# Attention sums turned by VectorE's block transposes instead of TensorE's, with four smaller moves beside it

## The reference

```python
q, k = _l2norm(proj(Wq)), _l2norm(proj(Wk))
v = proj(Wv)
attn = einsum('bhqd,bhkd->bhqk', q, k)
rel = pos[None, :] - pos[:, None]
mask = (rel < 0) | (rel >= WINDOW)          # WINDOW = 128
alibi = -abs(rel) * slopes[:, None, None]
attn = softmax(attn + where(mask, NEG_INF, alibi))
out = einsum('bhqk,bhkd->bhqd', attn, v).reshape(B, T, D)
x = _layernorm(x + einsum('btd,ed->bte', out, Wo))
h = gelu(einsum('bsd,hd->bsh', x, binarize(w1)) + b1)
x = _layernorm(x + einsum('bsh,dh->bsd', h, binarize(w2)) + b2)
```

## Time and profile before

| | |
|---|---|
| median of 3 runs | 369.94 us (369.66 to 370.51) |
| span of the profiled execution, first to last instruction | 368.4 us |
| TensorE busy | 353.2 us, 96% of the span, 4461 matmuls |
| VectorE busy | 308.7 us, 84% |
| ScalarE busy | 307.3 us, 83% |
| GpSimd busy | 285.4 us, 77% |
| granted TensorE clock, mean | 0.997 |

### The profile page before, as it was taken

How to read it: one execution, slowest core, us unless ns; L and a number is a source line. 1 busy time by engine, 2 the same in 40 slices (tenths; PEclk the granted TensorE clock), 3 DMA queues, 4 the chain that set the end, 5 groups by cost and what they waited for, 6 DMA issues and landing times. The chain is left out here.

```text
span 368.4 us, 13096 instructions
## 1 busy us (share of the span) xinstructions
PE 353.2 (96%) x4461; PEld 244.1 (66%) x4461; DVE 308.7 (84%) x771; ACT 307.3 (83%) x532; POOL 285.4 (77%) x440
## 2 busy tenths in 40 slices
PE   8789999999999999999999999999999999999992
PEld 5555676667766776776677677675666667667682
DVE  5977899898898898898899988879777887786775
ACT  3588888898898998898899999988888888887753
POOL 1188999889989999998999999757756856856433
PEclk9999999999999999999999999999999999999998
DMA  7678944744655646667767773303303513413113
GB/s 231 143 117 186 185 109 98 157 99 94 137 120 106 142 96 132 139 159 154 156 144 155 153 147 74 59 4 59 59 0 59 115 45 72 114 39 76 59 59 114
DMA packets 106884, 40.19 MB, mean 109 GB/s; under 512 B 92128, under 2 KB 105824, under 8 KB 106720
## 3 DMA queue, kind: packets, MB, share of 16 engines
q1 hardware_dynamic: 106848, 39.73, 49.6%
HBM read 12.72 MB, written 4.19 MB: 46 GB/s over the span
## 5 line engine op out<-in xcount | busy, mean ns | idle before, releaser
L1341 POOL TENSOR_SCALAR_AFFINE_SELECT prob<-prob 128x512 f32<-128x512 f32 x252 | 153.7, 646 | 11.1 <-ACT prob L700 11.1
L700 ACT ACTIVATE prob<-ps 128x1024 f32<-128x1024 f32 (+1 forms) x128 | 122.2, 1009 | 13.5 <-PE ps L390 13.4
L551 PE MATMUL ps<-yT,sgn 128*128 128x512 f16 x256 | 61.1, 379 | 0.0
L772 ACT ACTIVATE ps<-ps,bias,alpha 128x512 f32<-128x512 f32 x64 | 47.9, 750 | 15.6 <-PE ps L551 12.5
L421 PE MATMUL ps<-wqkv,xt 128*128 128x512 f32 x124 | 58.7, 596 | 1.2 <-DVE qkn L952 1.1
L411 PE MATMUL ps<-prob,vdiag 128*17 128x128 f32 x1024 | 51.3, 274 | 0.3
L411 PE MATMUL ps<-prob,vnext 128*17 128x128 f32 x992 | 49.9, 273 | 0.0
L1409 POOL TENSOR_TENSOR resid<-z,resid 128x256 f32 (+1 forms) x31 | 22.5, 726 | 29.9 <-DVE z L1173 29.9
L551 PEld LDWEIGHTS ps<-yT,sgn 128*128 128x128 f16 x256 | 25.0, 98 | 22.6
L390 PE MATMUL ps<-qkT 64*64 64x192 f16 (+2 forms) x1024 | 33.7, 248 | 2.8 <-DMA qkT<-parts 2.7
L454 PE MATMUL ps<-wo,oT 128*128 128x256 f32 x128 | 36.2, 405 | 0.1
(11 more groups left out here) (113 smaller groups left out, 690.2 us busy)
## 6 DMA issues: line engine op xcount, KB each, us to landing
xt<-in_xT SPq DMA_DIRECT2D x32, 128.0 KB, 2.1
resid<-in_x SPq DMA_DIRECT2D x32, 128.0 KB, 2.2
out_dram<-resid SPq DMA_DIRECT2D x7, 512.0 KB, 2.9
w<-in_w2T SPq DMA_DIRECT2D x1, 1024.0 KB, 7.7
w<-in_w1T SPq DMA_DIRECT2D x4, 256.0 KB, 3.3
w_nat<-in_w SPq DMA_DIRECT2D x4, 256.0 KB, 3.3
wqkv<-in_wqkvT SPq DMA_DIRECT2D x3, 256.0 KB, 3.9
qkT<-parts SPq DMA_TRANSPOSE x39, 4.3
```

What stands on the lines that cost most here:

```text
L551: mm = nc.tensor.matmul(ps[:, bank, :], sgn1[:, c, P * k:P * k + P], yT[:, par, a, c, :, :], start=(m == 0), stop=(m == 2 * DC - 1))
L700: nc.scalar.activation(to, scored, ACT.Exp, scale=QK_SCALE ** -2).then_inc(exp_done, 1)
L772: nc.scalar.activation(bank, bank, ACT.Gelu, bias=bias1[:, k:k + 1], scale=alpha1[:, k:k + 1]).then_inc(gelu_done, 1)
L1341: return nc.gpsimd.affine_select(out=at, in_=at, compare_op=ALU.is_ge, fill=0.0, base=-near, pattern=[[0, CH], [1 if near else -1, P]], ch ...
```

## The change

Five things change together.

1. **The sums are turned on VectorE.** `turn_sums` reads bank `OT` (128x512) and writes it to SBUF as `turned`, each 32x32 block transposed in place. `scale_sums` takes the reciprocal of the denominators, now from `turned`, multiplies (now SBUF by SBUF), and a second block transpose (128x256) makes `oT`, the left operand of the output projection. The feature order that this gives is taken up by a new order of `Wo`'s columns (`WO_SLOTS`), made on the host side with the other weight layouts. `turn_strips`, `turn_rows`, `take_strips` and `take_rows` are gone: six transposes and two copies a step.
2. **The output projection writes into bank `OT`**, into one of its two halves by the parity of the step, once the sums of the next block have been turned out of it. The weighted sums therefore wait for `resid_done` of the block before. In the last four blocks (`project_late`) it still uses `VO`. `oT` has two buffers.
3. **`double` moves from VectorE to ScalarE**, behind the root's logarithm and exponential, from step 4 on.
4. **GpSimd selects eight heads at once** (`cut_pair`): four selects of 128x1024 a step in place of eight of 128x512, each after both chunks' exponentials. The low halves come between the two pairs.
5. **One product makes both faded copies of the values** (`faded`) in place of two.

```diff
+WO_SLOTS = [SLOTS[CH * (2 * half + k) + m] for k in range(DC) for m in range(CH) for half in range(2)]
...
-        vdiag = sb("vdiag", [P, XS, H, HD + 1])
-        vnext = sb("vnext", [P, XS, H, HD + 1])
+        faded = sb("faded", [P, 2, XS, H, HD + 1])
         prob = sb("prob", [P, XS + 2, H, P])
-        strips = sb("strips", [P, CH, P])
+        turned = sb("turned", [P, H, 2 * HD])
         rden = sb("rden", [P, H])
-        otok = sb("otok", [P, D])
-        oT = sb("oT", [P, DC, P])
+        otok = sb("otok", [P, H // 2, 2, HD])
+        oT = sb("oT", [P, 2, DC, P])
...
                 if c == 0:
                     pe.wait_ge(v_ready, q + 2 if near else NB)
-                    count(pe, ot_ready, q)
+                    count(pe, sums_turned, q)
+                    count(pe, resid_done, q - 1 if not isinstance(q, int) or q < NB - 2 else 0)
-                if near:
-                    pe.wait_ge(cut_ready, (q + 1) * NC + c + 1)
-                else:
-                    pe.wait_ge(own_cut, c + 1)
+                if c % 2 == 0:
+                    if near:
+                        pe.wait_ge(cut_ready, (q + 1) * (NC // 2) + c // 2 + 1)
+                    else:
+                        pe.wait_ge(own_cut, c // 2 + 1)
                 for n in range(2 if near else 1):
                     for m in range(CH):
                         if n == 0:
-                            v, p = vdiag[:, slot, CH * c + m, :], prob[:, OWN_AT[slot], CH * c + m, :]
+                            v, p = faded[:, 0, slot, CH * c + m, :], prob[:, OWN_AT[slot], CH * c + m, :]
                         else:
-                            v, p = vnext[:, (slot + 1) % XS, CH * c + m, :], prob[:, NEAR_AT[(slot + 1) % 2], CH * c + m, :]
+                            v, p = faded[:, 1, (slot + 1) % XS, CH * c + m, :], prob[:, NEAR_AT[(slot + 1) % 2], CH * c + m, :]
...
-            def turn_strips(q):
-
-                pe.wait_ge(strips_ready, q + 1)
-                for c in range(NC):
-                    mm = nc.tensor.transpose(ps[:, OT, P * c:P * c + P], strips[:, c, :], id32[:])
-                mm.then_inc(otok_done, 1)
-
-            def turn_rows(q):
-
-                pe.wait_ge(onorm_done, q + 1)
+            def project_out(q, par):
+
+                pe.wait_ge(ot_ready, q + 1)
+                pe.wait_ge(sums_turned, q + 2)
                 for k in range(DC):
-                    mm = nc.tensor.transpose(ps[:, OT, P * k:P * k + P], otok[:, P * k:P * k + P], id32[:])
-                mm.then_inc(ot_done, 1)
-
-            def project_out(q, values, added=0):
-
-                pe.wait_ge(ot_ready, q + 1)
-                pe.wait_ge(v_ready, values)
-                count(pe, resid_done, added)
-                for k in range(DC):
-                    mm = nc.tensor.matmul(ps[:, VO, D:2 * D], oT[:, k, :], wo[:, k, :],
+                    mm = nc.tensor.matmul(ps[:, OT, D * par:D * par + D], oT[:, par, k, :], wo[:, k, :],
                                           start=(k == 0), stop=(k == DC - 1))
                 mm.then_inc(wo_done, 1)
...
+            def project_late(q):
+
+                pe.wait_ge(ot_ready, q + 1)
+                pe.wait_ge(v_ready, NB)
+                count(pe, resid_done, q if q > NB - 4 else 0)
+                for k in range(DC):
+                    mm = nc.tensor.matmul(ps[:, VO, D:2 * D], oT[:, q % 2, k, :], wo[:, k, :],
+                                          start=(k == 0), stop=(k == DC - 1))
+                mm.then_inc(wo_done, 1)
+
                 par = slot % 2
                 scores(i, 0, par, slot, both)
                 scores(i, 1, par, slot, both)
-                if out:
-                    project_out(i - 4, i + 1)
-                if strips:
-                    turn_strips(i - 3)
                 if amid:
                     amid()
                 if next3:
                     project_qk(i + 3, (slot + 3) % XS)
-                elif next1:
-                    project_v(i + 1, (slot + 1) % XS)
-                if before_rows:
-                    before_rows()
-                if strips:
-                    turn_rows(i - 3)
-                if next1 and next3 and not early:
+                if out:
+                    project_out(i - 4, par)
+                if before_values:
+                    before_values()
+                if next1 and not early:
                     project_v(i + 1, (slot + 1) % XS)
...
-            def take_strips(q):
-                act.wait_ge(pv_done, q + 1)
-                count(act, otok_done, q)
-                nc.scalar.activation(strips[:], ps[:, OT, :].rearrange("p (c t) -> p c t", c=NC),
-                                     ACT.Copy).then_inc(strips_ready, 1)
-
-            def take_rows(q):
-                act.wait_ge(ot_done, q + 1)
-                count(act, wo_done, q)
-                nc.scalar.activation(oT[:], ps[:, OT, 0:D].rearrange("p (k t) -> p k t", k=DC),
-                                     ACT.Copy).then_inc(ot_ready, 1)
-
+            def double(n, par):
+
+                done = n + 1
+                if not isinstance(n, int):
+                    done = act.to_reg(done)
+                act.wait_ge(lo_done, done)
+                nc.scalar.activation(parts[:, par, 0:H, 2:4, :], parts[:, par, 0:H, 0:2, :],
+                                     ACT.Copy).then_inc(parts_ready, 1)
+
...
+                if next2 and doubled:
+                    double(i + 2, par)
...
+            def turn_sums(q):
+
+                dve.wait_ge(pv_done, q + 1)
+                count(dve, onorm_done, q)
+                nc.vector.transpose(turned[:].rearrange("p b d -> p (b d)"), ps[:, OT, :]).then_inc(sums_turned, 1)
+
+            def scale_sums(q, par):
+
+                dve.wait_ge(sums_turned, q + 1)
+                nc.vector.reciprocal(rden[:], turned[:, :, HD]).then_inc(rden_done, 1)
+                dve.wait_ge(rden_done, q + 1)
+                count(dve, ot_ready, q)
+                nc.vector.tensor_tensor(otok[:].rearrange("p b a d -> p a b d"),
+                                        turned[:, :, 0:HD].rearrange("p (a b) d -> p a b d", a=2),
+                                        rden[:].rearrange("p (a b) -> p a b", a=2).unsqueeze(3).to_broadcast(
+                                            [P, 2, H // 2, HD]),
+                                        ALU.mult).then_inc(onorm_done, 1)
+                dve.wait_ge(onorm_done, q + 1)
+                count(dve, wo_done, q - 1)
+                nc.vector.transpose(oT[:, par].rearrange("p k t -> p (k t)"),
+                                    otok[:].rearrange("p b a d -> p (b a d)")).then_inc(ot_ready, 1)
+
             def outputs(q):
 
-                sums = ps[:, OT, :].rearrange("p (h d) -> p h d", d=32)
-                dve.wait_ge(otok_done, q + 1)
-                count(dve, onorm_done, q)
-                nc.vector.reciprocal(rden[:], sums[:, :, HD]).then_inc(rden_done, 1)
-                dve.wait_ge(rden_done, q + 1)
-                count(dve, ot_done, q)
-                nc.vector.tensor_tensor(otok[:].rearrange("p (h d) -> p h d", d=HD), sums[:, :, 0:HD],
-                                        rden[:].unsqueeze(2).to_broadcast([P, H, HD]),
-                                        ALU.mult).then_inc(onorm_done, 1)
-
-            def add_output(q):
+                turn_sums(q)
+                scale_sums(q, q % 2)
...
+                added = ps[:, VO, D:2 * D] if late else ps[:, OT, D * par:D * par + D]
+                nc.vector.tensor_tensor(resid[:, q, :], resid[:, q, :], added, ALU.add).then_inc(resid_done, 1)
...
                 v = ps[:, VO, 0:D].rearrange("p (h d) -> p h d", d=HD)
-                for to, at in ((vdiag, 0), (vnext, 1)):
-                    made = nc.vector.tensor_tensor(to[:, slot, :, 0:HD], v,
-                                                   fade[:, at, :].unsqueeze(2).to_broadcast([P, H, HD]), ALU.mult)
-                made.then_inc(v_ready, 1)
+                nc.vector.tensor_tensor(faded[:, :, slot, :, 0:HD], v.unsqueeze(1).to_broadcast([P, 2, H, HD]),
+                                        fade[:].unsqueeze(3).to_broadcast([P, 2, H, HD]), ALU.mult).then_inc(v_ready, 1)
...
                 par = slot % 2
+                turn_sums(i - 3)
                 if prev3:
                     round_of(i - 1, True, prev_ln)
                     normalise_rows(i + 2, par)
-                if out and not next3:
-                    add_output(i - 4)
-                if strips:
-                    outputs(i - 3)
-                if out and next3:
-                    add_output(i - 4)
+                scale_sums(i - 3, 1 - par)
+                add_output(i - 4, par)
                 if aside:
                     aside()
                 if next1 and not next3:
...
-                    if not double_first:
-                        fade_values(i + 1, (slot + 1) % XS)
-                if next2:
```

(30 more changed lines are left out.)

89 lines of the change are left out of this document (35 added, 54 removed).

## The result

The changed kernel takes 384.96 us, the median of 4 runs (384.62 to 385.43), beside 370.23 for the kernel before in the same session (369.66 to 372.72): ratio 1.0391, 95% interval [1.0356, 1.0426]. It is slower by 14.7 us. The profiled execution's span is 383.4 us in place of 368.4.

What follows compares the result with a forecast made beforehand. TensorE bounded the kernel before, three engines close behind; a ring through VectorE, ScalarE and GpSimd would bound the changed loop. Loop +1.5, small copies +1.5, last steps -0.5: +2.5 on 368.4, plus 1.5 to the median, 372.4 us; range 359 to 386.

Steps and rivals of the forecast that it cites:

- rival 3: Loop: L961 and half miss the ends of GpSimd's instructions in most steps; 7.75 us a step, 384 us; chance 0.15.
- TensorE, 6.50 a step: Loop: TensorE loses 0.65 us of transposes a step and gains nothing, 7.15 becomes 6.50.
- VectorE's load, 6.95 a step: Loop: 6.54 us, less 0.56 for double and 0.14 for one product, plus 1.11 for two transposes.
- GpSimd: Loop: a select of 1024 columns takes 1.11 us, about 1.08 at pace; 6.1 us a step with the low halves.
- ScalarE: Loop: loses copies of 0.58 us and smaller, gains double at 0.62; neutral off the step's end.
- The ring, 7.08 a step, mixed 7.3: Loop: half, logarithm, double, exponentials, selects, low halves, next half held by the long low half; mixed 7.1 to 7.65.
- rival 2: Loop: VectorE's load alone rules, waits do not lengthen with the select; 6.95 us a step, 362.5 us; chance 0.2.
- Loop in sum, +1.5 and +1.5 for the small copies: 25 steps of 7.3 instead of 7.24 us, +1.5; one more small ScalarE copy in five steps, +1.5.
- New waits: Loop: weighted sums wait for add_output, TensorE idles 0.6 to 0.8 us at no cost; coarser selects wanted a step later.
- The first steps: Ahead of step 4: the forecast's sum had no term for this stretch.
- The last steps, -0.5 between -3.9 and +2.2: From 222.29 to 257 us: TensorE sheds 3.9 us; VectorE's last two blocks bring 2.2 against 1.6 free.
- Rival 1: Loop: TensorE stays the bound, held instructions fall into GpSimd's gaps; steps of 6.5 to 6.6, 351 us; chance 0.15.

Runs made afterwards that it cites:

- tiny_turns_all: The changed kernel with both VectorE block transposes cut to 32 columns from block 3 on, loop included: 380.91 us.
- fine_start: The changed kernel with selects of four heads in steps 0 to 4 only, eight heads from step 5 on: 379.66 us.
- tiny_turns_end: The changed kernel with both VectorE block transposes cut to 32 columns for the last six blocks only: 382.06 us.
- early_turns: The changed kernel with VectorE turning the sums of blocks 30 and 31 earlier in the written-out end: 387.57 us.
- before_eight: The kernel before with only the eight-head selects, low halves between the pairs: 390.75 us.
- scale_first: The changed kernel with VectorE's loop order altered: first turn, reciprocal and otok, then root products and qkn, then the second transpose: 403.72 us.
- four_double_back: The changed kernel with four-head selects and the doubling copy back on VectorE: 402.03 us.
- tiny_selects: The changed kernel with every GpSimd select cut to 8 of 128 columns a head: 357.64 us.

## Why the prediction was right and wrong

The range (359 to 386) held the time, near its slow end; the likeliest value was 12.6 us short. That it was held is luck: the range reached past 380 only for rival 3, whose mechanism did not come, and the loss came from two stretches that the sum had at nothing and at -0.5. By its own steps:

- **TensorE, 6.50 a step**: right. Freed from the selects, it ran at 6.61 (6.51 in steps 8 to 24).
- **VectorE's load, 6.95 a step**: right in size, 173.22 / 25 = 6.93, which is no test, as this busy time does not fall when 0.74 us of work are taken out. The pair of transposes was put at 1.11 and measured 0.705 + 0.445 = 1.15; the single fade product at 0.69, measured 0.68. The statement of the Trainium skill that a transpose streams one element per cycle and lane ("Vector Engine (DVE) Microarchitecture Reference", "The reshape front-end and per-opcode configuration") stands with these rows.
- **GpSimd**: select 1.11 alone and 1.08 at pace; measured 1.129 in the mean and 2.13 / 2 = 1.07. Right.
- **ScalarE**: `double` at 0.62, measured 0.61. Right.
- **The ring, 7.08 a step, mixed 7.3**: right in length, wrong in its last link. It took 7.22 in the steady steps, 7.37 in the mean. That holds and hand-overs set it and not VectorE's load was forecast against rival 2, and tiny_turns_all shows it: 0.74 us less load, 0.06 us less time. But the prediction closed the ring through `half`, held by the long low half. In the steady steps `half` takes its free 0.18 us; the ring closes through the hold of `otok` and VectorE's list behind it, the second transpose included. In steps 4 to 6 it was held, for up to 1.19 us; in steps 25 to 28 it takes 0.26, but the logarithm behind it started when ScalarE was done with its exponentials (208.57), so it did not wait for `half` there.
- **Loop in sum, +1.5 and +1.5 for the small copies**: +3.2 measured against +3.0, in part by luck. The steady steps lost 0.9 us in all, the four with the small copy another 0.9, and 1.4 came in steps 4 to 7, still in the wake of the start, which the prediction did not price.
- **New waits**: TensorE's gap ahead of the weighted sums was put at 0.6 to 0.8 and measured 0.73, but ended by the wrong engine. The view of the waits gives 18.6 us to GpSimd's selects and 3.8 to the residual's addition. With the transposes cut the share turns over (19.3 us behind the addition), so the two come nearly together; the size was right, the name was not. The coarser selects were not "wanted a whole step later": the weighted sums start at 155.84, and the pair of selects is over at 155.77.
- **The first steps: no term at all. This failed**, by 5.6 us. The prediction wrote that `nt_b` and `rnorm` "depend on each other, so behind running selects each costs a whole one", and then applied it to the loop only, where little of it came true. It applied ahead of step 4, where the four selects stand back to back and the chain has nothing to fall between. fine_start, which undoes only that, gives 5.3 us back, 2.9 of them ahead of step 4. The other 2.8 go with TensorE's gap behind the values and its clock, which had no term either.
- **The last steps, -0.5 between -3.9 and +2.2. This failed**, by 6.6 us and outside its bounds. The sum had 2.2 us of new VectorE work against 1.6 us free in the last 15, as if VectorE's idle time there could be filled to the end; and it let TensorE's 3.9 us count as a gain. In fact VectorE's busy time, holds included, rose by 7.8 us over the tail (31.06 to 38.84), from 84% to 90% of it, while TensorE shed only 1.7 of its 3.9 us, at a granted clock of 0.92 (34.47 us against 31.52 at 1.00 for the same matmuls). tiny_turns_end gives back 4.5 of the 6.1 us; early_turns, another order of the same work, gave none back. The clock had no term in the sum at all.
- **Rivals**: the 384 us of rival 3 came out, but not its mechanism; its 7.75 a step did not appear in this kernel. It did appear in its neighbours: before_eight at 7.91, scale_first at 8.03, four_double_back at 8.21. The forecast step was right by a margin that small edits undo. Rival 1 is what tiny_selects is.

Where the gain of TensorE's 0.65 us a step went: it became the gap ahead of the weighted sums (0.73 us a step), because the bound moved from TensorE to the ring through VectorE, ScalarE and GpSimd.

## What to carry to other kernels

When work moves off the engine that bounds a loop, price the stretches outside the loop by the same rows: fill and drain have other neighbours (here four selects back to back) and no slack to average over, and 12 of 15 us were lost there. A gap on TensorE is to be priced with the clock behind it, not as idle time alone. Where a chain of small dependent VectorE products with two SBUF inputs runs beside GpSimd, each may cost one whole GpSimd instruction (4.23 us for four of them beside selects of 1.07, 2.41 beside selects of 0.6), so the length of that instruction counts and not only GpSimd's load; where other work lies between, as in this loop, shorter selects gave 0.05 us a step, because more instructions met one. A sum round a repeating step always comes out, so each link of a ring is to be checked by whether its instruction takes longer than when free. VectorE's busy share says nothing of its load until the holds are taken off.

## What the runs showed of the hardware

- The block transposes, 128x512 out of PSUM and 128x256 within SBUF, took 698 to 718 and 445 to 448 ns in all 32 blocks, also beside a select (154.85, within the select that began at 154.49); `otok`, the product of two SBUF tensors between them, ranged from 424 to 1182.
- The hold has a price on the other side too: a pair of selects takes 2.13 us, but 2.32 where `otok` meets its first select, in the changed kernel and in tiny_turns_all alike. It is the second select that grows, to 1.27 us.
- Behind a gap of 2.94 us (granted clock 0.62) TensorE took 2.91 us for 64 matmuls that take 1.94 in the loop, behind one of 1.92 us (0.60) 3.10; but behind 2.67 us at 248.81 the projection kept its 1.10, and behind 1.70 us in tiny_turns_end the 64 matmuls kept their 1.94. The gaps of 0.7 us once a step in the loop left the granted clock at 1.00.
- Removing 0.74 us of work a step from an engine without idle time changed neither its busy time (94.07 and 94.02 us in 100) nor, by more than 0.06 us, the step.
